# Opening of a fused attention and node-graph kernel: filling products, the node weights' folding moved and split, bias products mixed in, load order changed

## What is computed

```python
x = L0_attn_hidden_states                      # 16 x 256 x 128, float32
x = x + attn(_layernorm(x))
x = x + ffn(_layernorm(x))

# attn
h = _rms(x, attn_norm_w)
q, k, v = h @ Wq, h @ Wk, h @ Wv               # 64, 64, 128 wide, 4 heads
glog = log_sigmoid(h @ Wgk1 @ Wgk2 + bgk2) / 16
o = _gla_chunk(q, k, v, glog, 4)               # chunks of 64: masked scores and a carried state
o = _rms(o, gnorm_w) * silu(h @ Wg)
x2 = o @ Wo + x
n = _rms(x2, mlp_norm_w)
return x2 + silu(n @ W_gate) * (n @ W_up) @ W_down

# ffn: nodes[-1] = its input; for each of 6 nodes c
q = ew[c, 0] * (nodes[in_q] @ We[eq] + be[eq]) # k and v alike
o = _mha(q, k, v, Wq[c], Wk[c], Wv[c], Wo[c])  # 8 heads
nodes[c] = act_w[c] * o + q
return _layernorm(nodes[5])
```

## Time and profile before

| | us |
|---|---|
| median of 3 runs | 1197.93 |
| lowest and highest | 1196.95 and 1199.43 |
| the profiled execution | 1199.51 |
| its span, first to last instruction | 1197.70 |
| TensorE busy in the span | 1126.4 (94%) |
| VectorE busy | 846.3 (71%) |
| ScalarE busy | 738.8 (62%) |
| GpSimd busy | 427.9 (36%) |
| mean granted TensorE clock | 0.96 |

### The profile page before, as it was taken

One profiled execution on the slowest core, in us unless ns is written; L12 is line 12 of the kernel. 1 busy time (PEld: TensorE's weight loads), 2 busy tenths in 40 slices (PEclk: granted clock), 3 DMA queues, 4 the chain that ended last, 5 costly groups with the idle time before them and its releaser, 6 DMA issues.

```text
span 1197.7 us, 28000 instructions
## 1 busy us (share of the span) xinstructions
PE 1126.4 (94%) x10236; PEld 786.0 (66%) x10236; DVE 846.3 (71%) x1857; ACT 738.8 (62%) x1597; POOL 427.9 (36%) x848
## 2 busy tenths in 40 slices
PE   5889888897899999999999999999999999999995
PEld 3575555554577677777777777777777777777773
DVE  4547777764678777777777787777777777777783
ACT  4434555553376667667667666776676676676674
POOL 3301111112333333333333368733333333333375
PEclk8688999897899999999999999999999999999998
DMA  8000000003565676675666667766656656667640
GB/s 218 1 1 1 1 0 0 0 1 53 76 86 86 90 95 83 90 99 84 94 94 83 94 92 101 101 91 94 87 90 94 89 90 94 89 89 95 88 69 24
DMA packets 83549, 87.02 MB, mean 73 GB/s; under 512 B 11482, under 2 KB 69342, under 8 KB 83422
## 3 DMA queue, kind: packets, MB, share of 16 engines
q1 hardware_dynamic: 82254, 83.17, 48.0%
q0 software_dynamic: 848, 2.11, 1.1%
q10 hardware_dynamic: 320, 0.05, 0.0%
HBM read 6.51 MB, written 2.10 MB: 7 GB/s over the span
## 4 chain that ended last, share of the span: by engine, by line
PE 80%; ACT 6%; POOL 5%; DVE 5%; issue 3%; DMA 1%; SPq 0%; ACTq 0%; DVEq 0%; POOLq 0%
PE bank L1137 72%; PE bank L1446 3%; PE bank L1453 3%; ACT region L627 1%; ACT region L634 1%; DVE region L1050 1%; DVE region L937 1%; PE bank L1419 1%; DVE region L935 1%; POOL out L597 1%; POOL region L422 1%; POOL xall L424 1%; POOL region L420 1%; POOL hl L539 1%; DMA wa<-in_L_attn_Wg 1%
## 5 line engine op out<-in xcount | busy, mean ns | idle before, releaser
L739 ACT ACTIVATE region<-bank 128x512 f32<-128x512 f32 x768 | 416.8, 595 | 263.4 <-PE bank L1137 251.5
L1050 DVE TENSOR_REDUCE region<-bank 128x2 f32<-128x512 f32 x768 | 491.9, 681 | 78.7 <-PE bank L1137 78.4
L1137 PE MATMUL bank<-st 48*128 48x256 f32 x3072 | 376.2, 352 | 5.2 <-DVE region L1050 5.1
L1137 PEld LDWEIGHTS bank<-st 48*128 48x128 f32 x3072 | 266.8, 190 | 84.2 <-issue 30.9
L1137 PE MATMUL bank<-region 128*32 128x256 f32 (+5 forms) x3586 | 260.1, 377 | 4.4 <-issue 1.9
L539 POOL TENSOR_TENSOR hl<-qk,one_col 128x512 fp32r<-128x512 f32 x96 | 99.8, 1039 | 411.1 <-ACT qk L706 411.1
L1137 PEld LDWEIGHTS bank<-region 128*32 128x32 f32 (+3 forms) x3586 | 130.4, 115 | 97.4 <-issue 29.4
L1137 PE MATMUL bank<-mst,ones 64*128 64x512 bf16 x768 | 151.1, 389 | 0.2 <-ACT region L739 0.2
L542 POOL TENSOR_TENSOR hl<-qk,hl 128x512 fp32r<-128x512 f32 x96 | 122.5, 1276 | 7.5
L1066 DVE COPY mrows<-bank 24x256 bf16<-24x256 bf16 x96 | 26.7, 279 | 98.9 <-PE bank L1419 98.7
L1137 PE MATMUL bank<-region,wgu 128*128 128x512 f32 (+1 forms) x96 | 60.7, 763 | 18.8 <-DVE region L974 17.7
(11 more groups left out here) (194 smaller groups left out, 1465.6 us busy)
## 6 DMA issues: line engine op xcount, KB each, us to landing
st<-hl SPq DMA_DIRECT2D x576, 128.0 KB, 4.5
mst<-mrows SPq DMA_DIRECT2D x192, 6.0 KB
out<-xall POOLq DMA_DIRECT2D x15, 128.0 KB, 3.8
xall<-in_L_attn_hidden_states SPq DMA_DIRECT2D x1, 768.0 KB, 6.7
cst<-in_constants SPq DMA_DIRECT2D x1, 514.5 KB, 3.8
xT<-in_L_ffn_Wq SPq DMA_DIRECT2D x1, 384.0 KB
xT<-in_L_ffn_Wk SPq DMA_DIRECT2D x1, 384.0 KB
xT<-in_L_ffn_Wv SPq DMA_DIRECT2D x1, 384.0 KB
```

The costliest lines, as they stand in the source:

```text
L739: act.activation(to, x_bank(x, k, e)[:, :].rearrange("p (j q) -> p j q", j=2), ACT.Exp).then_inc(B["exp_ok"], 1)
L1050: dve.tensor_reduce(mx[s.n % 2][:, to:to + 2], s_bank(s, k, e)[:, :].rearrange("p (j k) -> p j k", j=2), AX_X, ALU.max, negate=True).then_ ...
L1137: return pe.matmul(o, w, x, start=start, stop=stop, skip_group_check=skip)
```

## The change

- Fillers: `warm(n)` issues n products of 128x128 ones by 512 columns in bfloat16, whose result nobody reads: 16 and 8 around the gate weights' preparation, 6, 6 and 4 in slot 0, 4 in slot 1, 3 ahead of z in slots -1, 0 and 1, 3 ahead of the projections in slots 0 and 1.
- Folding: `fold_weights` now runs on TensorE behind slot 0 for nodes 0 to 3, with the 18 bias products among them; the transposes of nodes 0 and 1 stand in slot 0 ahead of the mean product; nodes 4 and 5 and the six second bias products stand in slot 1 behind the key transposes. VectorE scales nodes 0 to 3 and multiplies the biases behind slot 0; nodes 4 and 5 and the rest of `biases` stand in slot 1 between L820 and L829. The `wgu` scaling moves behind slot 0 as well.
- TensorE waits in slot 1 for the bias multiply ahead of at, for four scaled nodes ahead of g, for five ahead of kv, for six behind the first two score products.
- Opening: x is loaded ahead of the constants; the `cols` loads move to ScalarE's queue; `wz` is scaled ahead of `wa` and z waits for it alone; the table load on ScalarE comes ahead of its first copy, and one in slot -1 is left out; GpSimd sets `ones` and `mst` ahead of its loads.

```diff
@@ sync
+            sp.dma_start(xall[:, 0:TPI, :], x_d[:, 0:TPI, :]).then_inc(L["x_first"], 16)
             sp.dma_start(cst[:, :], consts).then_inc(L["const_in"], 16)
-            sp.dma_start(xall[:, 0:TPI, :], x_d[:, 0:TPI, :]).then_inc(L["x_first"], 16)
-            sp.dma_start(cols[:, 0:1], col(a["L0_attn_attn_norm_w"])).then_inc(L["cols_in"], 16)
-            sp.dma_start(cols[:, 1:2], col(a["L0_attn_mlp_norm_w"])).then_inc(L["cols_in"], 16)
-            for h in range(GH):
-                sp.dma_start(cols[DV * h:DV * h + DV, 2:3], col(a["L0_attn_gnorm_w"])).then_inc(L["cols_in"], 16)
@@ gpsimd
+            pool.memset(ones[:, :], 1.0).then_inc(S["ones_ok"], 1)
+            for n in range(2):
+                pool.memset(mst[n][:, :, :], 0.0).then_inc(S["ones_ok"], 1)
@@ scalar
+            act.dma_start(cols[:, 0:1], col(a["L0_attn_attn_norm_w"])).then_inc(L["cols_in"], 16)
             act.dma_start(bgk[:, :], a["L0_attn_bgk2"].partition_broadcast(P)).then_inc(L["gk_in"], 16)
+            act.dma_start(cols[:, 1:2], col(a["L0_attn_mlp_norm_w"])).then_inc(L["cols_in"], 16)
+            for h in range(GH):
+                act.dma_start(cols[DV * h:DV * h + DV, 2:3], col(a["L0_attn_gnorm_w"])).then_inc(L["cols_in"], 16)
+            act.preload_act_table_set(LOGS)
...
-                if isinstance(i, int) and i == 1:
-                    transposed_weights()
...
-                act.preload_act_table_set(LOGS)
+                if i is not None or j is not None:
+                    act.preload_act_table_set(LOGS)
...
+                    if isinstance(i, int) and i == 0:
+                        act.wait_ge(S["we_t"], 1)
+                        act.activation(beT, bank[6][:, 3 * D:3 * D + EDGES], ACT.Copy).then_inc(S["be_c"], 1)
+                        transposed_weights(0)
+                        transposed_weights(1)
...
-            slots(act, first)
+            slots(act, first, {0: later_weights})
@@ vector
                     dve.tensor_tensor(x2, quads(5), xn, ALU.add).then_inc(A["x2_ok"].sem, 1)
+                if isinstance(i, int) and i == 1:
+                    scale_fold(4)
+                    scale_fold(5)
+                    biases()
...
-            slots(dve, first, {1: biases, 2: last_bias})
+            slots(dve, first, {0: scale_weights, 2: last_bias})
@@ tensor
+            def warm(n, to=7):
+
+                pe.wait_ge(S["ones_ok"], 1)
+                for _ in range(n):
+                    mm(quads(to), ones[:, :], ones[:, :].unsqueeze(1).to_broadcast([P, 4, P]))
+
+            warm(16)
...
+            warm(8)
...
                 if k is not None:
+                    if isinstance(k, int) and k == 0:
+                        pe.wait_ge(S["bias_c"].sem, S["bias_c"].at(0))
...
                 if i is not None:
+                    if isinstance(i, int) and i == 0:
+                        warm(6)
                     pe.wait_ge(A["qke_ok"], i + 1)
+                    if isinstance(i, int) and i == 1:
+                        pe.wait_ge(S["fold_ok"], 4)
...
+                if isinstance(i, int) and i == 0:
+                    warm(6)
                 if isinstance(i, int) and i == 1:
-                    fold_weights()
+                    fold_products(4)
+                    fold_products(5)
+                    for c in range(NODES):
+                        n = mm(bank[6][:, 64 + c:65 + c], wo_raw[:, c, :], bprod[:, c, 2:3])
+                    n.then_inc(S["bo_ps"].sem, 1)
+                    pe.wait_ge(S["fold_ok"], 5)
...
+                    if isinstance(i, int) and i == 0:
+                        warm(4)
+                    if isinstance(i, int) and i == 1:
+                        pe.wait_ge(S["fold_ok"], NODES)
+                        warm(4)
...
                 if f is not None:
+                    if isinstance(f, int) and f in (0, 1, 2):
+                        warm(3)
                     pe.wait_ge(A["hT_ok"], f + 1)
...
                     if i is None:
-                        pe.wait_ge(S["wa_ok"], 1)
+                        pe.wait_ge(S["wz_ok"], 1)
...
                 if f is not None:
+                    if isinstance(f, int) and f in (1, 2):
+                        warm(3)
+                    if i is None:
+                        pe.wait_ge(S["wa_ok"], 1)
...
             def fold_weights():
 
+                pe.wait_ge(S["be_c"], 1)
+                pe.wait_ge(A["msl_ok"].sem, A["msl_ok"].at(0))
+                for b, nodes in enumerate(((0, 1), (2,), (3, 4), (5,))):
+                    fold_products(b)
+                    fold_transposes(b + 2)
+                    for c in nodes:
                         for j in range(3):
+                            e = GRAPH[c]["e"][j]
+                            k = mm(bank[5][:, 3 * c + j:3 * c + j + 1], stacked_heads(j, c), beT[:, e:e + 1])
                 k.then_inc(S["bias_ps"].sem, 1)
...
-            slots(pe, first, {1: biases, 2: last_bias})
+            slots(pe, first, {0: fold_weights, 1: folded, 2: last_bias})
```

More of the change, by code:

```diff
@@ L85, in mlp_bank, with fold_bank @@
     return first + (0, 1, 0, 0, 1, 1, 0, 1)[m]
+def fold_bank(c):
+    return (3, 0, 3, 0, 3, 7)[c]
 class Event:
@@ L717, in gate_tanh, with transposed_weights, later_weights @@
                 act.activation(eg[0:MROWS[m], m % 2, :], bank[mlp_bank(m, j)][0:MROWS[m], :], ACT.Tanh, scale=0.5).then_inc(A["eg2_ok"], 1)
[L719 to L727, removed]
+            def transposed_weights(c):
+                act.wait_ge(S["we_t"], c + 1)
+                if c >= 2:
+                    act.wait_ge(S["fold_ps"], c - 1)
+                act.activation(weT[:, c % 2, :], bank[6 + c % 2][:, 0:3 * D], ACT.Copy).then_inc(S["we_c"], 1)
+            def later_weights():
+                for c in range(2, NODES):
+                    transposed_weights(c)
             def exps(x, k):
@@ L1246, in first @@
                     n.then_inc(A["v_ps"], 1)
+                if isinstance(i, int) and i == 0:
+                    pe.wait_ge(L["nodew_in"], 16 * 6)
+                    pe.transpose(bank[6][:, 3 * D:3 * D + EDGES], be_rows, ident[0:EDGES, 0:EDGES])
+                    pe.wait_ge(S["heads_ok"], 1)
+                    fold_transposes(0)
+                    fold_transposes(1)
                 if i is not None:
@@ L1352, in biases, with fold_transposes @@
-            def biases():
-                for c in range(NODES):
-                    for j in range(3):
-                        e = GRAPH[c]["e"][j]
-                        k = mm(bank[7][:, 3 * c + j:3 * c + j + 1], stacked_heads(j, c), beT[:, e:e + 1])
+            def fold_transposes(c):
+                if c >= 2:
+                    pe.wait_ge(S["we_c"], c - 1)
+                for j in range(3):
+                    k = pe.transpose(bank[6 + c % 2][:, j * D:(j + 1) * D], we_raw[:, GRAPH[c]["e"][j], :], ident)
+                k.then_inc(S["we_t"], 1)
@@ L1358, in biases, with folded @@
                 k.then_inc(S["bias_ps"].sem, 1)
-                pe.wait_ge(S["bias_c"].sem, S["bias_c"].at(0))
-                for c in range(NODES):
-                    k = mm(bank[7][:, 64 + c:65 + c], wo_raw[:, c, :], bprod[:, c, 2:3])
-                k.then_inc(S["bo_ps"].sem, 1)
+            def folded():
+                pe.wait_ge(S["bo_ok"].sem, S["bo_ok"].at(0))
             def last_bias():
```

64 lines of the change are left out of this document (24 added, 40 removed).

## The result

The changed kernel takes **1185.57 us** (median of 4 runs, 1178.75 to 1187.35) beside 1198.43 for the kernel before (1196.95 to 1199.43): a ratio of 0.9885, interval 0.985 to 0.9921, 12.9 us less. A fifth execution of it took 1185.68. The forecast was 1193.4 with a range from 1181.9 to 1199.5: the direction and this wide range held, but the saving is 2.9 times the 4.5 us that I had forecast, and 1185.57 lies outside the forecast's own range of 1189 to 1198.

The account below looks back on a forecast made before the run. TensorE at its low 1.2 GHz clock in the opening, with waits for weights, fold and biases, was taken as the bound. Terms -3.6 - 6.1 + 10.0 - 3.8 - 1.0 = -4.5 gave 1193.4 us; own range 1189 to 1198, wide 1181.9 to 1199.5.

Parts of the forecast that it names:

- the first rival: Fillers and the mixture hold the clock through the block and slot 1: -16.0 us, 1181.9; chance 18%.
- Start: Before slot 0: earlier weights and fillers at the high clock start slot 0 at 17.2, not 20.8: -3.6 us.
- Slot 0: Fillers hold the clock in slot 0, so scores and outputs come earlier: 22.4 rather than 28.5 us, -6.1.
- The block: Fold and bias products moved between slots 0 and 1 cost 8.5 to 15.5 us; clock lost partway: +10.0.
- Slot 1: Fold and bias wait leave slot 1, but the clock falls before the scores and stays low: 38.1 us, -3.8.
- Slot 2: Slot 2 begins at the high clock, so at and g cost less: -1.0 us; its low stay in the gates remains.
- Sum up to slot 3: All terms from the start through slot 2 together: -4.5 us.
- the second rival: Loop slots losing the clock elsewhere take back most of the gain, or the block's low price does: about 1198; 17%.
- The third rival: Clock not lifted in time; fillers cost 0.4 us each and outlast idle time, block 15.5: +16, 1213.9; 9%.

Follow-up runs that it names:

- typical run: The changed kernel run once more with nothing edited, for a second profile: 1186.22 us, ratio 0.9901.
- first profile of after: The profiled execution of the changed kernel in its first set of runs, the fastest of the four: 1178.75 us.

## Why the prediction was right, and where its sizes were off

**The mechanism was right, the size was not.** The change is worth what the fillers do to TensorE's clock: without them 0.6 us are left. But every term up to slot 3 save the start came out better than forecast, and 3.8 us more came from behind it, which the forecast had at nothing. The median of 1185.57 lies nearer to the first rival's 1181.9 than to the forecast's 1193.4, and it is the wide range, not the forecast's own, that holds it.

**Start: -3.6 forecast, -2.4 and -3.0 measured.** What was off is the landing of the column loads, which I had there by 9 to 11, covered or at 0.7. The last landed at 12.3: `wz`, expected at 10.3, ran at 12.35 in one profile. The other terms held: with the first column apart slot 0 begins at 16.97, 0.2 from the forecast of 17.2. That Wg is issued earlier (at 3.18 rather than 5.96, 2.8 us and not 3.3) gained nothing to see, as the old order gives 17.23.

**Slot 0: -6.1 forecast, -7.3 measured.** The chain was the forecast's; the outputs took 3.39 in place of 5.73. But they began 12.0 us into the slot, where I had VectorE's masks and states end at 14.2. I took nothing off these for GpSimd; measured, the state operations took 1.87 us rather than 2.77, and were over before GpSimd's scalings began.

**The block: +10.0 forecast, +7.7 measured.** I had bounded it by 8.5 and 15.5 and taken a loss partway; in no profile did the clock fall within it. The pure price was 0.8 too high as well, most of it in the bias products: 0.20 us each and not 0.227. A loss came right behind the block instead, in slot 1's entry: 3.4 us low in three of the nine profiles that have the 18 products and no fillers there. It cost 1.4 to 1.5 us (slot 1 36.6 beside 35.3, 28.4 beside 26.9) where I had 2.0.

Twelve transposes lie in the block and it ran at 1.00 throughout, with the one-column products among them or behind them. The Trainium skill (TensorE: Matmul & The Clock Gate, Part 4) says that a transpose doesn't count as busy for the clock as a product does. The trace neither shows nor refutes that, since products stand between the transposes; the 13 us that I had drawn from it for the block did not come.

**Slot 1: 38.1 forecast, 36.6 in the typical run, 28.2 in the fastest.** This is the forecast's main step and it held: a fall ahead of the scores and no way back before the projections (low from 60.6 to 81.1, forecast from about 13 to 30 us into the slot, measured from 14.0 to 34.4). Masks came at 13.6 and 15.0 us against 14.7. The 28.2 of the fastest run is the slot of the first rival (28.6): by the times it was reached in one of the ten executions (the others took 1184 to 1189.5); with more fillers each profile has it (28.4 to 26.9).

**Slot 2: -1.0 forecast, -1.6 measured**, as it begins high and has only the low spell of its own.

**Sum up to slot 3: -4.5 forecast, -9.5 in the typical run.** That is +0.6 from the start, -1.2 from slot 0, -2.3 from the block, -1.5 from slot 1 and -0.6 from slot 2.

**Behind slot 3: nothing forecast, -3.8 measured.** I had considered this only as a way to lose (the second rival), so this part of the gain is luck. The loop and node part move by 2 to 4 us with where the clock happens to fall. Over all profiles the node part takes 921.8 to 922.3 us with 10.2 low us in stretches that begin in its first 50, 923.9 to 924.4 with 17.1, and 925.9 with 20.5; the three profiles with one loop slot of 32.0 or 32.1 us (before, without the fillers, more fillers in slot 1) are all of the middle kind. In the change it came in as a gain, in the kernel with fillers at the entry of slot 1 as a loss.

**The third rival** (the clock still low as slot 0 begins, and fillers at half the clock that outlast the idle time) came in no profile. The slot 0 of 30.4 us with the fillers in the loop is another thing: the clock was high for its first 13.6 us and fell in a wait for VectorE that the prediction doesn't have. The block behind it ran high (7.7 us).

**Open.** Why the low stretch in slot 1 lasts 3.4 us in one execution and 20.5 in the others isn't settled. The fall came 15.7 us into the slot in the one and 14.0 in the other, and the three fillers ahead of z (64.95 to 66.4) ran just ahead of the rise in the first. The other profiles with the folding moved and no added fillers in slot 1 line up with this: with a fall 12.3 to 14.4 us into the slot the stretch is 20.5 us long in six of six, with one at 15.4 (one product in place of the 18) it is 13.7, with 15.7 it is 3.4. So a later fall went with a shorter stretch, but no run moved the fall alone. Nor is it shown which executions lose a further stretch in the loop.

## What to carry to other kernels

Look at the granted clock before counting idle time: here TensorE looked 90% busy through 24 us of slot 0 and ran at half speed, and fillers in the standstills of 1.5 us there gave most of 8.8 us. Fill every standstill ahead of narrow products, not only the first; fillers at the start alone gave about nothing. Where the clock falls in a place that was filled, look for the wait in front of the fall: here it was once VectorE, held up beside GpSimd. Where such a clock decides, compare stretches of two profiles with each other, but judge an edit by the median of many executions, since a stage that nobody touched may take back or add 2 to 4 us.

## What the runs showed of the hardware that I had not expected

- The clock held at 2.4 GHz through the 7.7 us of products, transposes and one-column products in all profiles here, whether they were mixed or apart. In three of nine it fell 0.3 to 0.8 us behind them, as in before it fell at 87.8, 0.1 us behind the same 18 one-column products by themselves.
- VectorE's small operations stretch beside GpSimd's large ones. The first profile of after, timeline of VectorE and GpSimd, first such an operation by itself, then in slot 1:

```profile
8.10 0.17 DVE L945 SCALAR_TENSOR_TENSOR region<-region 128x8 f32<-128x8 f32 x1
...
57.26 1.04 POOL L528 TENSOR_TENSOR region<-region 128x512 f32<-128x512 f32 x1 [6.13 <-DVE region L947]
57.29 1.03 DVE L945 SCALAR_TENSOR_TENSOR region<-region 128x8 f32<-128x8 f32 x1
...
58.25 1.27 POOL L531 TENSOR_TENSOR xall<-region,xall 128x512 f32<-128x512 f32 x1
...
58.35 1.20 DVE L947 SCALAR_TENSOR_TENSOR region<-region 128x8 f32<-128x8 f32 x1
```

  An operation of 0.17 us takes 1.03 and 1.20 us while GpSimd runs its two, and ends as each of them ends. About 2 us of the chain that leads to slot 1's masks is this, and it lies in the very stretch in which TensorE stands still.
- The same on a larger scale delays slot 0's states. A 64x128 operation (L899) that takes 0.34 us elsewhere took 5.77 us with the fillers in the loop, from 28.07 to 33.84, while GpSimd ran on without a gap until 33.69. In the other three profiles with the delay, too, the first of the four operations ends 0.15 us behind the last of GpSimd's scalings. Why the one at 28.07, begun among GpSimd's copies ahead of the scalings, was held already, and the one at 27.63 in after wasn't, isn't shown.
